# Twenty-eight raw pairs in the list stage, 74 mixed pairs, 92 fixes beside 84 pairs, and a key table

## The reference

```python
hx = jnp.einsum('ni,rio->rno', x, weight)
msg = hx[edge_type, src]
agg = jax.ops.segment_sum(msg, dst, num_segments=num_nodes)
node_repr = agg * 0.5 ** 0.5 + h_bias
node_repr = node_repr + (x @ loop_weight) * 0.5 ** 0.5
y = x + node_repr
out = (y - mean(y)) / sqrt(var(y) + 1e-5)
```

## Time and profile before

| | us |
|---|---|
| median of 3 runs (777.53 to 779.74) | 777.81 |
| the profiled execution, its own time | 779.01 |
| its span | 777.2 |
| PE busy, 4550 matmuls | 650.5 (84%) |
| DVE busy | 569.1 (73%) |
| ACT busy | 476.6 (61%) |
| POOL busy | 422.2 (54%) |

### The profile page before, as it was taken

The page is one execution under the profiler, slowest core; times in us unless marked ns, Lnnn a source line. Parts: engine busy times, 40 slices in busy tenths (PEclk is TensorE's granted clock), DMA queues, the critical chain, the costliest instruction groups (busy, mean ns, idle before and its releaser), DMA issues. The chain is left out here.

```text
span 777.2 us, 15732 instructions
## 1 busy us (share of the span) xinstructions
PE 650.5 (84%) x4550; PEld 566.4 (73%) x4550; DVE 569.1 (73%) x1903; ACT 476.6 (61%) x1143; POOL 422.2 (54%) x426
## 2 busy tenths in 40 slices
PE   1388646588999999999999999999999999999630
PEld 1166326478999999899999999878787878878410
DVE  7949989646566656565665689988989889889730
ACT  2668902455665565556556667787787777777730
POOL 1000008167777777777776700766766666767363
PEclk9999767999999999999999999999999999999955
DMA  5301006566777777776776689899989999998621
GB/s 160 124 28 55 0 16 194 188 211 195 263 251 249 221 250 258 236 252 224 239 252 227 214 267 268 279 308 323 317 298 306 345 318 317 336 304 280 221 81 46
DMA packets 78900, 173.41 MB, mean 223 GB/s; under 512 B 25744, under 2 KB 41426, under 8 KB 78817
## 3 DMA queue, kind: packets, MB, share of 16 engines
q1 hardware_dynamic: 59233, 125.16, 48.0%
q0 software_dynamic: 19584, 47.23, 18.8%
HBM read 100.47 MB, written 78.20 MB: 230 GB/s over the span
## 5 line engine op out<-in xcount | busy, mean ns | idle before, releaser
L750 DVE TENSOR_TENSOR xt_low<-xt_ps,xt_high 128x512 fp32r<-128x512 f32 x241 | 165.1, 685 | 130.0 <-ACT xt_high L962 129.7
L1140 PE MATMUL y_ps<-w_high,xt_high 128*128 128x256 f32 x752 | 213.5, 284 | 0.0
L1140 PE MATMUL y_ps<-w_high,xt_low 128*128 128x256 f32 x752 | 213.1, 283 | 0.0
L1140 PE MATMUL y_ps<-w_low,xt_high 128*128 128x256 f32 x752 | 213.0, 283 | 0.0
L529 POOL DMA_INDIRECT gathered<-in_x,src_at x105 | 113.1, 1077 | 144.0 <-DVE edge_at L734 112.3
L962 ACT ACTIVATE xt_high<-xt_ps 128x512 fp32r<-128x512 f32 x241 | 142.2, 590 | 63.8 <-PE xt_ps L1108 63.6
L997 ACT ACTIVATE y_out<-y_ps,rstd 128x256 f32<-128x256 f32 x376 | 156.7, 471 | 14.1 <-DMA out_rows<-y_out 13.5
L558 POOL DMA_INDIRECT out_rows<-y_fix,fix_at x99 | 98.7, 996 | 95.8 <-ACT y_fix L1036 73.2
L1140 PEld LDWEIGHTS y_ps<-w_high,xt_low 128*128 128x128 f32 x752 | 143.8, 191 | 8.4
L1108 PE MATMUL xt_ps<-ident,x_in 128*128 128x128 f32 (+1 forms) x784 | 120.0, 277 | 34.9 <-DMA x_in<-in_x 15.5
L1140 PEld LDWEIGHTS y_ps<-w_low,xt_high 128*128 128x128 f32 x752 | 144.2, 192 | 0.2
(11 more groups left out here) (164 smaller groups left out, 914.9 us busy)
## 6 DMA issues: line engine op xcount, KB each, us to landing
x_in<-in_x SPq DMA_DIRECT2D x97, 512.0 KB, 5.0
out_rows<-y_out SPq DMA_DIRECT2D x97, 512.0 KB
message_in<-message_rows SPq DMA_DIRECT2D x99, 128.0 KB
keys<-padded_dst SPq DMA_DIRECT2D x13, 508.0 KB, 7.0
w_rel<-in_L_gnn_weight SPq DMA_DIRECT2D x1, 2048.0 KB, 14.3
gathered<-in_x,src_at POOLq DMA_INDIRECT x105, 4.0
message_rows<-message_out,edge_at POOLq DMA_INDIRECT x105
y_fix<-out_rows,fix_at POOLq DMA_INDIRECT x99
```

Source lines behind the costliest of these rows:

```text
L750: nc.vector.tensor_tensor(xt_low[:, q % XT_RING, :], xt_ps[q % 2][:, :], xt_high[:, q % XT_RING, :].bitcast(F32), ALU.subtract).then_inc(l ...
L1140: return nc.tensor.matmul(to, xt[:, at_row:at_row + P], w, start=start, stop=stop)
```

## The change

`schedule`: HOLD 8 becomes 28, 4 lead pairs stand for 6, 74 mixed mains for 82, 6 for 8 after them; then 84 mains carry 92 fixes, so that eight slots have two fixes; then six empty slots and 7 fixes alone. The first message is at slot 32, the last at 156, the first fix at 165, the last main at 248 again. PE runs the second fix of a slot behind the multiplication.

`startup`: each group step is followed by two held pairs instead of one, and the sort of group k-2 follows the count of group k. The weights of the main pairs are made by DVE before its first masks. The lane masks of groups 8 to 13 (42 of 98) are made by POOL.

The 14 held blocks are stored raw at once. In the mixed stage each is loaded back into `late` four slots ahead of message 4+3b, measured by DVE and scaled by ACT in the slots after it, and stored again.

The keys of the fixes: a table `key_table` in F32 is written once to DRAM, 128 keys a window, and `load_keys` broadcasts from it in runs of 4 KB, where it took 508-byte runs before; ACT's `fill_keys` (L1025) goes.

POOL: 8 early fix gathers instead of 12, between the last four scatters; then each step gathers group n+2 ahead of scattering group n (before: scattered n, then gathered n+3). Fixes 92 to 98 now wait for the last store.

```diff
-HOLD = 8
-PAUSE = 8
-TAIL = 8
+HOLD = 28
+LEAD = 4
+MIXED = 74
+PAUSE = 6
+TAIL = 7
+POOL_LANES = 8
...
-    AHEAD = 12
+    AHEAD = 8
+    late_at = {g_at[4 + 3 * b]: b for b in range(HELD)}
...
-    EARLY = FT - 5
+    EARLY = (FT - TAIL) // 4 * 4
...
         def startup(step_f, step_s, step_m, late):
-            sorts = 0
-            for k in range(GROUPS):
-                step_f(k)
-                while sorts < GROUPS and 2.5 + 4 * sorts < 4.9 * (k - 3):
-                    step_s(sorts)
-                    sorts += 1
-                if 0 <= k - late - 2 < HOLD:
-                    step_m(k - late - 2)
+            for k in range(GROUPS + 4):
+                if k < GROUPS:
+                    step_f(k)
+                if 2 <= k < GROUPS + 2:
+                    step_s(k - 2)
+                for m in range(2 * (k - 1 - late), 2 * (k - late)):
+                    if 0 <= m < HOLD:
+                        step_m(m)
...
+            def load_late(b):
+                if b >= 2:
+                    sp.wait_ge(late_stored[b % 2], 16 * (b // 2))
+                sp.wait_ge(stored[b % BLOCK_RING], 16 * (b // BLOCK_RING + 1))
+                sp.dma_start(late[:, b % 2, :, :], block_rows(out, b)).then_inc(late_loaded[b % 2], 16)
+
+            def store_late(b):
+                sp.wait_ge(held_normed, 2 * b + 2)
+                sp.dma_start(block_rows(out, b), late[:, b % 2, :, :]).then_inc(late_stored[b % 2], 16)
...
-                sp.dma_start(keys[:, u % 2, :, 1:P], padded_dst[u * UNIT * RUN + 1:(u + 1) * UNIT * RUN + 1].rearrange("(t k) -> t k", k=RUN).partition_broadcast(P)).then_inc(keys_loaded[u % 2], 16)
+                sp.dma_start(keys[:, u % 2, 0:size, :].rearrange("p t k -> p (t k)"),
+                             key_table[u * UNIT:u * UNIT + size, :].rearrange("t k -> (t k)").partition_broadcast(P)).then_inc(keys_loaded[u % 2], 16)
...
+                if s - 7 in late_at:
+                    store_late(late_at[s - 7])
+                if s + 4 in late_at:
+                    load_late(late_at[s + 4])
...
+            pool.wait_ge(nodes_ready, 2)
+            for k in range(POOL_LANES, GROUPS):
+                for c in range(k * GROUP, (k + 1) * GROUP):
+                    last = nc.gpsimd.tensor_scalar(lane_mask(c), lane_iota[:, :], node_lo[:, c:c + 1], None, ALU.is_equal)
+                last.then_inc(lo_built_pool, 1)
...
             for n in range(FGROUPS):
+                for i in group_tiles(n + 2):
+                    if i == 4 * (n + 2) and n >= 2:
+                        pool.wait_ge(fix_scattered[(n - 2) % 4], fix_gathers(n - 2))
+                    gather_fix(i)
                 for i in group_tiles(n):
                     pool.wait_ge(f_normed, i + 1)
                     scatter_fix(i)
-                for i in group_tiles(n + 3):
-                    if i == 4 * (n + 3) and n >= 1:
-                        pool.wait_ge(fix_scattered[(n - 1) % 4], fix_gathers(n - 1))
-                    gather_fix(i)
...
             for s in range(HOLD, len(slots)):
-                kind, n, f = slots[s]
+                kind, n, fs = slots[s]
                 turn(s + 2)
-                if f is not None:
-                    fix(f)
+                if fs:
+                    fix(fs[0])
...
                     multiply(s, offsets)
+                for f in fs[1:]:
+                    fix(f)
```

225 lines of the change are left out of this document (120 added, 105 removed).

## The result

| | before | after |
|---|---|---|
| median, us | 778.58 (4 runs, 777.53 to 779.74) | 757.73 (4 runs, 755.83 to 758.89) |
| ratio | | 0.973 [0.9702, 0.9757] |
| span of the profiled execution, us | 777.2 | 755.3 |

The kernel is 2.7% faster, 20.9 us. The forecast was 5%, 738, with a range of 723 to 755: the side was right, the size was not, and the range missed. The profiled span is 755.3 where the prediction's sum was 737.7, so 17.6 us are to be found.

A forecast was written before the change was run, and what follows sets the result against it. Four stages in sequence, each priced on its last engine (PE, then POOL at the end): gain -8.7 lists, +37.7 to the first fix, +12 fix stage, -1.6 tail, giving 738 us; range 723 to 755.

The forecast's parts named there:

- the returning blocks: Mixed stage: 14 blocks cost DVE some 2.2 us each and ACT as much; bounds 0 and 1 us each, taken as nothing.
- Start of the full steps: List stage: DVE's bias wait, weights, two mask groups, sums, first sort group and third mask group put it at 36.3 us.
- "I take nothing" for POOL's masks: List stage: 42 masks on POOL, priced at 0.30 us each, 12.6 us where POOL is idle, add nothing.
- a rival, at 12 us: List stage: POOL's masks block DVE for all their 12.6 us before the first sort, giving 750; chance 0.13.
- Length of a step: List stage: one count, one sort and two held pairs take PE 6.60 us; twelve full steps are 79.2.
- Message pair: Mixed stage: each costs PE 2.31 us beside main pairs at 2.10; 53 of them, 122.4 us, precede the first fix.
- a race with POOL: Mixed stage: POOL at 395 and PE at 398 are level, so 3 us are added, bounds 0 and 10.
- POOL's pace: Mixed stage: a step costs POOL 5.31 us and PE 5.24, so the two are level.
- ACT's 13.5 us for the stores of held blocks: Mixed stage: this wait goes, because held blocks leave `y_out` while the lists are made.
- the rival on the slow side: Returning blocks stall SP's queue, so x loads come late; 787 at 3.5 us a block; chance of slower 0.04.
- the fix stage: 84 slots at 2.92 us, eight second fixes at 1.3, less 2 for the keys: 253.7 us.
- The rivals at 750 and 752: 750: POOL's masks block DVE, chance 0.13; 752: gathers and scatters 5% slower in the mixed stage, 14 us, chance 0.12.

The follow-up runs named there:

- first variant: The changed kernel with all 14 groups of lane masks made on DVE and none on POOL; 755.36 us.
- Moving the read: PE reads a message pair's two weight offsets one slot earlier: 748.49 us on the changed kernel, 770.18 us on the kernel before.
- work alone: The changed kernel with DVE and ACT still measuring and scaling the returning blocks, but without the 28 transfers that load and store them; 755.52 us.

## Why the prediction was wrong in size

The path was right, stage by stage; terms of the sum were not. POOL's masks and the returning blocks were taken at nothing, the price of a list step was misread, and message pairs kept a mean price while their order changed.

**Start of the full steps**, +2.5: the term "I take nothing" for POOL's masks. The trace had a row of another instruction, a select of 0.30 us that ran alone; a mask takes 0.61 alone and 1.08 beside DVE, so that 42 of them took POOL 44 us and not 12.6. The mechanism was named as a rival, at 12 us; it costs 1.3 to 2.0 (first variant), and the rest is when the bias landed. The wait for it, taken as 4, was 4.08.

**Length of a step**, +5.7, and it was legible in the trace of before. The prices 1.03, 0.99 and 2.29 were taken from the weight loads, and 0.26 was deducted as a wait. That was a wait of the loads, which run ahead of the matmuls. PE's own rows in the kernel before, at the same place as the earlier trace rows:

```profile
50.13 1.35 PE L1171 MATMUL y_ps<-column_of,y_fix 128*128 128x394 f16 x7 [0.70 <-ACT column_of L967]
51.32 1.12 PE L1177 MATMUL y_ps<-gathered,keys 128*128 128x318 f16 x7
52.28 0.60 PE L1108 MATMUL xt_ps<-ident,x_in 128*128 128x128 f32 x4
```

The next count starts at 54.69, without a wait. So the prices were 1.19, 0.96 and 2.41, 6.97 us a step. In the changed kernel the starts are 1.18 (95.78 to 96.96), 0.95 and 2.40 apart, 6.92 a step. Over twelve steps and the rest this is 4 us. The first of the full steps adds 1.6: its count takes 2.46 us where the others take 1.34, because PE ran at the lower of its two clock levels (the granted clock is 0.50 from 38.8 to 41.0 us, 1.00 from 47.3 to 54). PE had waited 4.59 us just before; but after 2.89 us it was 2.46, too, and after 3.04 us in the version with the bias from ACT's queue it was 1.34, so the length of that wait alone doesn't decide.

**Message pair**, +6.4, or +9.4 without the 3 us that were added for a race with POOL: 2.31 us was a mean over all of them, which hid that some cost more. With main pairs in twos, 12 message pairs of before follow another one, of the changed kernel 16, since 74 mains stand between 53 messages and not 82. By PE's timelines the gaps there are 13.0 us in all before and 16.8 after, some 1.1 each; four more made 3.8 us. (Moving the read gave back only 10.5 in each of the two kernels, 0.66 a place in the changed one, since it opens smaller gaps elsewhere.) The prediction changed the mix and kept the price. The other term is the returning blocks, "bounds 0 and 1 us each, I take nothing": measured 3.1 (work alone) to 6.6 in all, 0.2 to 0.47 a block. The bounds were right, the choice wrong. Without the return the stage is 303.6, still 2.8 above the 300.8 that the sum has without the race; so 6.6 and 2.8 make the 9.4. That the 2.8 are the four more gaps fits by size, but no run has the changed kernel's mix with 12 of them.

**POOL's pace** was weighed as level with PE's, and that proved right only once PE was relieved: then both end at 300 us. The 3 us for the race were counted without cause, since PE was behind.

**Right**, for the reason given: ACT's 13.5 us for the stores of held blocks went; 9.65 us of idle time before PE's resumption stayed; 22 issues in 28.4 us; nobody waited on SP's queue, so the rival on the slow side had no ground. **Right by luck**: the fix stage, with 2.83 and 2.1 for 2.92 and 1.3; and the wait for the bias, 4 us taken between 0 and 4.6 without a row for it, measured 4.08.

**The range** was too narrow on one side: all three misses went the same way. Two took the cheap end of an unknown cost, the step's price was misread. The rivals at 750 and 752 had the masks and the stage separately; their sum wasn't among the cases.

## What to carry to other kernels

Take an engine's step from the starts of its own instructions, never from its weight loads, and check the price on a stretch where it is the bound. A mean price holds only while the mix and the order hold: look for the gap that only some of the instances have, and ask what stands in the queue there that the trace doesn't list. Where several costs are unknown, put the sum of their middle values in the sum and not that of their low ends.
